# A decoder layer on one core: gathering the routed tokens one tile ahead, through a buffer of their own

## The reference, cut to what matters

```
x = x + attention(layernorm(x), w_atten, w_proj)          # 4 x 512 tokens of 512 numbers
x = x + cross(layernorm(x), ctx, Wq, bq, Wk, bk)
x = x + ffn(layernorm(x), ...)

def ffn(x, ...):                                          # float32 throughout
    shared = silu(x @ Ws_gate) * (x @ Ws_up) @ Ws_down    # 704 hidden, every token
    scores = softmax(x @ W_router)                        # 8 experts
    topk_vals, topk_idx = top_k(scores, 2)                # two experts for each token
    h = silu(x @ We_gate[e]) * (x @ We_up[e])             # 352 hidden, for each expert e
    y_all = h @ We_down[e]
    return shared + sum over the two chosen e of topk_vals * y_all[e]
```

## Time and profile before

| | us |
|---|---|
| median of 3 runs (1032.37 to 1033.8) | 1032.44 |
| profiled execution | 1030.51 |
| its span | 1028.3 |
| PE busy in the span | 975.6 (95%) |
| DVE busy | 613.8 (60%) |
| ACT busy | 485.9 (47%) |
| POOL busy | 183.3 (18%) |

### The profile page before, as it was taken

The page is one execution under the profiler, slowest core; times in us unless marked ns, Lnnn a source line. Parts: engine busy times, 40 slices in busy tenths (PEclk is TensorE's granted clock), DMA queues, the critical chain, the costliest instruction groups (busy, mean ns, idle before and its releaser), DMA issues.

```text
span 1028.3 us, 18243 instructions
## 1 busy us (share of the span) xinstructions
PE 975.6 (95%) x6186; PEld 783.0 (76%) x6186; DVE 613.8 (60%) x1621; ACT 485.9 (47%) x1274; POOL 183.3 (18%) x209
## 2 busy tenths in 40 slices
PE   8988999999999999998999999999899999999998
PEld 6457666767676776765776889888888889899997
DVE  5698777776876767867354674432442444334565
ACT  1568665656656666568512411333343344332221
POOL 3222211221111211100000010111121111113342
PEclk9999999999999999999999999999999999999999
DMA  9665844458424574285500312824424452424564
GB/s 241 107 104 76 155 89 63 63 100 241 76 36 63 103 209 69 43 201 191 198 11 22 112 33 78 290 87 151 160 88 141 146 163 83 147 72 134 170 194 148
DMA packets 69835, 124.88 MB, mean 121 GB/s; under 512 B 6336, under 2 KB 22720, under 8 KB 69760
## 3 DMA queue, kind: packets, MB, share of 16 engines
q1 hardware_dynamic: 63296, 104.76, 41.1%
q0 software_dynamic: 5600, 18.35, 6.0%
q10 hardware_dynamic: 864, 0.79, 0.5%
HBM read 70.14 MB, written 28.57 MB: 96 GB/s over the span
## 4 chain that ended last, share of the span: by engine, by line
PE 77%; DMA 9%; DVE 7%; issue 3%; ACT 2%; POOL 1%; SPq 0%; DVEq 0%; POOLq 0%; ACTq 0%
PE ps L1347 22%; PE ps L1357 12%; PE ps L1113 7%; DMA routed_x<-xn_d,table_cur 5%; PE ps L1262 5%; PE ps L1165 5%; PE ps L1204 5%; PE ps L1152 3%; PE ps L1138 3%; PE ps L1188 3%; DMA ks<-rope_a 2%; PE ps L1365 2%; PE ps L1335 2%; PE ps L1054 2%; PE ps L1224 2%
## 5 line engine op out<-in xcount | busy, mean ns | idle before, releaser
L1520 DVE CUSTOM_DVE_ANT_0 probs<-ps,mask 128x128 f32<-128x128 f32 (+3 forms) x256 | 122.6, 486 | 70.8 <-PE ps L1152 39.8
L864 ACT COPY probsT<-ps 128x128 f32<-128x128 f32 (+3 forms) x256 | 108.5, 425 | 114.9 <-PE ps L1165 71.8
L856 ACT ACTIVATE probs<-probs,nb 128x128 f32<-128x128 f32 (+3 forms) x256 | 146.3, 572 | 23.4 <-DVE nb L1525 22.9
L1152 PE MATMUL ps<-ks,qs 96*128 96x256 f32 (+2 forms) x256 | 128.3, 505 | 13.1 <-DVE mx L1520 10.7
L1165 PE MATMUL ps<-ident,probs 128*128 128x128 f32 x640 | 113.8, 277 | 2.3 <-ACT probsT L864 2.1
L965 ACT ACTIVATE sg<-ps 128x352 f32<-128x352 f32 x69 | 32.0, 464 | 170.8 <-PE ps L1347 170.7
L1804 DVE TENSOR_TENSOR hidden<-sg,ps 128x352 f32<-128x352 f32 x69 | 35.8, 519 | 110.1 <-ACT sg L965 110.0
L1165 PEld LDWEIGHTS ps<-ident,probs 128*128 128x128 f32 x640 | 79.6, 142 | 28.6 <-issue 19.4
L1357 PE MATMUL ps<-d_hi,h_hi 128*128 128x512 f32 (+1 forms) x207 | 88.2, 426 | 1.3 <-DVE h_lo L1808 1.3
L1152 PEld LDWEIGHTS ps<-ks,qs 96*128 96x128 f32 x256 | 49.0, 192 | 48.4 <-DVE mx L1520 22.5
L1808 DVE TENSOR_TENSOR h_lo<-ps,h_hi 128x384 fp32r<-128x384 f32 x69 | 38.4, 557 | 77.3 <-ACT h_hi L969 76.8
(11 more groups left out here) (187 smaller groups left out, 2078.7 us busy)
## 6 DMA issues: line engine op xcount, KB each, us to landing
gu_raw<-in_we SPq DMA_DIRECT2D x10, 1408.0 KB, 6.7
y_d<-y_sb SPq DMA_DIRECT2D x37, 256.0 KB, 2.5
shared_x<-xT_d SPq DMA_DIRECT2D x32, 256.0 KB, 2.8
qs<-rope_b SPq DMA_DIRECT2D x30, 256.0 KB, 5.7
ks<-rope_b SPq DMA_DIRECT2D x30, 256.0 KB, 5.2
d_raw<-in_we SPq DMA_DIRECT2D x10, 512.0 KB, 8.2
attT<-in_wpT SPq DMA_DIRECT2D x4, 1024.0 KB, 8.1
acc<-in_x SPq DMA_DIRECT2D x4, 1024.0 KB, 10.4
```

The source lines that it names most:

```text
L856: nc.scalar.activation(pr, pr, ACT.Exp, bias=nb[:, n % 2, h:h + 1], scale=SCALE, accum_out=sums[:, n % 2, h:h + 1]).then_inc(exp_done, 1)
L864: nc.scalar.copy(probsT[n % 2][:, h, 0:w], ps[:, T_BANK + h % 2, 0:w]).then_inc(pT_done, 1)
L1152: nc.tensor.matmul(ps[:, S_BANK + h % 2, 0:w], stacks[G % 2][0][:, h, i * P:(i + 1) * P], stacks[G % 2][1][:, h, 0:w], start=True, stop=Tr ...
L1520: nc.vector.tensor_tensor_reduce(probs[n % TT][:, h, 0:w], ps[:, S_BANK + h % 2, 0:w], mask[:, TOKENS - w:], 1.0, LOWEST, ALU.add, ALU.max ...
```

## The change

A second buffer, `arrived`, takes the gathered tile. POOL gets a new step, `hand_over(j)`: it waits for the gather of tile j to land and for TensorE to have turned tile j - 1, and copies `arrived` to `routed.x` (128x512 float32). The gather of tile j + 1 is issued right behind that copy, where before it was issued behind the turning of tile j. TensorE waits for the copy.

```diff
+        arrived = sb("arrived", [P, DIM])
...
+        x_arrived = sem("x_arrived")
...
                 nc.gpsimd.tensor_copy(table_cur[:], table[:, bass.ds(j, 1)]).then_inc(cur_copied, 1)
                 pool.wait_ge(cur_copied, j + 1)
+                if not isinstance(j, int) or j:
+                    pool.wait_ge(routed.x_loaded, j)
                 pass_wait(pool)
-                pool.indirect_dma_start(out=routed.x[:], out_offset=None, in_=xn3_d,
+                pool.indirect_dma_start(out=arrived[:], out_offset=None, in_=xn3_d,
                                         in_offset=bass.IndirectOffsetOnAxis(ap=table_cur[:, 0:1], axis=0))\
-                    .then_inc(routed.x_loaded, 16)
+                    .then_inc(x_arrived, 16)
+
+            def hand_over(j):
+
+                pool.wait_ge(x_arrived, j * 16 + 16)
+                if not isinstance(j, int) or j:
+                    pool.wait_ge(routed.x_turned, j)
+                pass_wait(pool)
+                nc.gpsimd.tensor_copy(routed.x[:], arrived[:]).then_inc(routed.x_loaded, 1)
 
             gather(0)
+            hand_over(0)
+            gather(1)
             total = pool.value_load(first_i[0:1, EXPERTS:EXPERTS + 1], min_val=EXPERTS * LEAST, max_val=ROUTED_TILES)
-            with pool.Fori(0, total) as j:
-                pool.wait_ge(routed.x_turned, j + 1)
-                pass_wait(pool)
+            with pool.Fori(1, total) as j:
+                hand_over(j)
                 gather(j + 1)
+            hand_over(total)
...
             def turn(path, j):
 
-                pe.wait_ge(path.x_loaded, j * 16 + 16)
+                pe.wait_ge(path.x_loaded, j + 1)
```

## The result

| | before | after |
|---|---|---|
| median of 4 runs | 1032.40 us (1030.5 to 1033.8) | 1014.21 us (1013.74 to 1018.33) |
| profiled execution | 1030.51 | 1014.37 |
| its span | 1028.3 | 1012.2 |
| first to last turn of the routed pass | 272.07 | 257.27 |
| idle of TensorE in front of a turn | 14.0, 8 times | none |

The change made the kernel faster, by 1.7%: the ratio of the runs is 0.983, with a 95% interval of 0.980 to 0.986. The forecast was 1017.5 us in a range of 1011.5 to 1023.5. Beside the first four experiments one execution of the kernel before took 1384.0 us, at a mean granted clock of 0.65 where the others have 0.98 to 0.99; it is in none of the ratios.

What follows compares the result with a forecast made beforehand. The prediction took the stage to be bound by TensorE, with eight holes waiting for gathers. 15.1 + 3.2 - 4.3 = 14.0 us off the profiled 1030.51 gave 1016.5, taken as 1017.5; range 1011.5 to 1023.5.

Steps and rivals of the forecast that it cites:

- The holes: TensorE's eight waits for gathers before a turn in the routed pass all go, winning 15.1 us.
- The clock behind them: Stretches at lower granted clock behind two of the holes return to full speed, winning 2 x 1.6 = 3.2 us.
- POOL's copies: 38 copies on POOL of 0.61 us each lie beside TensorE's 6.71 us per tile and cost nothing by themselves.
- The price on VectorE: The copy delays VectorE's weight rests at experts' first tiles, 7 x 0.61 = 4.3 us on TensorE's path.
- The sum: Holes plus clock less the price on VectorE: 15.1 + 3.2 - 4.3 = 14.0 us won.
- From the profile to the median: 1016.5 from the profiled execution, 1018.4 with the median's 1.93 us added; 1017.5 taken for the whole kernel.
- the likeliest case: The forecast case for the whole kernel, spanning 1015 to 1020 us, chance 0.55.
- The spare time of 2.7 us: Even the longest gather landing, 7.6 us, is copied 2.7 us before its turn on TensorE is due.
- no price: Rival: POOL waits or the copy slips past VectorE's four rests, so nothing is lost there; about 1013.5 us, chance 0.17.
- a dear copy: Rival: POOL's copy costs near 1.275 us, paid at eight expert starts; about 1023 us, chance 0.14.
- holes in part: Rival: gathers behind weight loads still land late, half of TensorE's holes stay; about 1025 us, chance 0.07.
- slower than before: Rival: the copy holds VectorE's two instructions behind every turn; about 1050 us at a 1.8 us copy, chance 0.04.

Runs made afterwards that it cites:

- the first four experiments: copy_later, copy_wide, copy_latest and copy_no_advance, run together; the kernel before took 1033.0 us there.
- before_no_loads: The kernel before, with the seven weight loads of the routed pass cut to a few KB: 1011.5 us.
- copy_wide: The changed kernel with the copy made 128x1024 instead of 128x512, the second half zeros: 1023.1 us.
- copy_later: The changed kernel, with the hand-over waiting until VectorE has made the low part of the tile before, instead of until TensorE has turned it: 1011.0 us.
- rest_moved: The changed kernel, with the fourth gate and up weight rest at an expert's first tile moved behind hidden_low on VectorE: 1009.0 us.
- copy_latest: The changed kernel, with the hand-over waiting until VectorE has issued the low part of the hidden tile of the tile before: 1010.9 us.
- copy_no_advance: The changed kernel with buffer and copy kept, but the gather of tile j + 1 waiting again until TensorE has turned tile j: 1036.7 us.

## Why the prediction was right

Point by point, by its own steps. The mechanism came as forecast; the size of the price on VectorE came out right partly by luck.

- *The holes, 15.1 us*: 14.51 at the seven loads and 1.0 at expert 0, 15.5. That they are the gather beside a load, and not something else in those tiles, is shown by before_no_loads; that nothing else is late there, by tiles of 6.70 us after.
- *The clock behind them, 3.2 us*: 3.4 by the turns. Two of the eight holes were followed by a stretched tile; in other runs of before the number probably differs, since their mean clock goes with their time, but only one execution has a trace of its turns, so this stays argued.
- *POOL's copies, 0.61 us each, hidden*: a median of 0.612 measured, and the other tiles still take 6.7 us. Taking the price from a memset of that size plus what a read adds was right to a hundredth. The 768 ns of the Trainium skill for a tight loop (GPSIMD Engine Reference, section 3.1) do not fit this copy; the rough line rate for one input of its section 4.1 (Engine selection) fits, with 0.43 us for the 512 further elements of copy_wide.
- *The price on VectorE, 4.3 us*: 4.23. The total is right because misses cancel in it. I had counted eight places less one like expert 5's. Expert 5 was held like the others, and expert 0, which I had counted, went free, so that it was seven after all. The hold of a rest is 0.41 us, not 0.61 (the stretched rest takes 1.30 us, not 1.5). And the first rest starts 0.1 to 0.3 us later than before, for the register load ahead of it takes 4.5 us over the seven experts instead of 3.5, a term that the prediction did not have. 7 x 0.41 + 1.0 = 3.9 of the 4.2. The path is also wider than I had it: I followed the delay through `xT_lo` alone, and TensorE waits for `hidden`, behind the same rests, too. The Trainium skill (GPSIMD Engine Reference, section 8, Key points) has the engines contend where VectorE reads two SBUF inputs; the rests of 3.30, 3.71 and 4.14 us in copy_later, the change and copy_wide agree, and so does `hidden`, with one input in PSUM, which keeps its 0.52 us beside the copy in rest_moved.
- *The sum, 14.0*: 14.8 in the pass. The profiled execution gained 16.1, of which 1.3 lie outside the pass and belong to no step.
- *From the profile to the median*: the medians differ by 18.2 us, 4 more than the sum. I had put the median of the kernel after 1.0 us over what the sum gives for its profiled execution, and it came 0.2 under its profiled execution (1014.37 and 1014.21), while the kernel before has its median 1.9 over. That is 1.2 of the 3.3 us by which 1014.2 lies under the forecast; 0.8 are the pass, and 1.3 lie outside it. It is inside the range, and 0.8 under the 1015 at which the likeliest case's own range began. The low end of that range was itself reckoned wrong: 1012.9 less 1.9 is 1011.0, not 1011.5.
- *The spare time of 2.7 us*: in the change the slowest gather landed in 6.8 us, and every copy ended at least 3.5 us ahead of its turn. The limit itself was not reached.

The rivals: no price (against it, 4.2 us), a dear copy (0.61, not 1.275), holes in part (none) and slower than before (`xT_lo` is 0.68 us beside the copy as ever) all fall by the trace; copy_wide shows what a copy of 1.04 us would have cost.

## What to carry to other kernels

Read a wait for a transfer by its places, not its total: eight of 38 gathers made all of it, seven of them beside one large load, and a start a tile earlier cured them for the price of a copy. When a cure puts work on an idle engine, ask what it meets on the others: the copy cost TensorE nothing in ordinary tiles, and 4.2 us at seven expert starts, most of it through VectorE's instructions that read two tiles of SBUF. Such a collision can be taken away from either side by one line of order, which here took another 3.9 us from the pass on POOL's side (median 1011.0) or 5.9 on VectorE's (1009.0).

## What the runs showed of the hardware that was not expected

- A GpSimd copy among VectorE's instructions with two SBUF inputs holds the next of them for its own length less 0.2 us (0.41 for 0.61, 0.84 for 1.04), and is itself held until the running one ends; the table copy of 0.18 us became 0.84 in this way.
- A gather started 1.1 us ahead of a 2.1 MB load landed in 4.0 us, and one 5.8 us behind it in 4.4 (copy_latest); started 2.0 us behind it, it took 7.3. With the loads cut to a few KB, none of 655 to 900 us took over 4.3.
- An idle time of 1.44 us, at expert 3 of copy_wide, was followed by 3.5 us of matmul pairs at 0.8 instead of 0.48 us (granted clock 0.67 from 753 to 757.5 us), while the hole of 2.32 us before the turn of 777.27 in the kernel before was followed by a tile of 6.76 us at a granted clock of 1.00.
- What the collision costs depends on the phase: at the starts of experts 1 to 7 the change held VectorE for 0.41 us in all seven cases, and copy_no_advance, whose copy comes 1.8 us ahead of the turn at expert 1, by 0.1 us at most.
- A register load on VectorE's queue took 0.50 to 0.53 us when it started 0.95 us behind a gather's issue (copy_later), and 1.02 to 1.04 when it started 1.9 us behind (copy_wide, five cases). The cause is open.
